# Pairing score units on TensorE in a fused cross-attention kernel, with a new order on every engine

## The reference

```python
q = _split_heads(hidden_states @ w_q, HEADS)
k = _split_heads(text @ w_k, HEADS)
v = _split_heads(text @ w_v, HEADS)
out_text = _merge_heads(_sdpa(q, k, v))
k_ip, v_ip = _split_heads(ip_h @ w_k_ip, HEADS), _split_heads(ip_h @ w_v_ip, HEADS)
out_ip = _merge_heads(_sdpa(q, k_ip, v_ip, mask=mask_ip))
out = (out_text + IP_SCALE * out_ip) @ w_out + b_out + residual
```

## Time and profile before

| | |
|---|---|
| median of 3 runs | 820.23 us (819.54 to 821.26) |
| the profiled execution | 820.14 us, its span 818.3 us |
| busy in the span | PE 795.8, DVE 676.2, POOL 627.7, ACT 541.3 us |
| stage 7 (its first pair to the next stage's) | 422.47 to 467.61 us |

### The profile page before, as it was taken

How to read it: one execution, slowest core, us unless ns; L and a number is a source line. 1 busy time by engine, 2 the same in 40 slices (tenths; PEclk the granted TensorE clock), 3 DMA queues, 4 the chain that set the end, 5 groups by cost and what they waited for, 6 DMA issues and landing times.

```text
span 818.3 us, 12921 instructions
## 1 busy us (share of the span) xinstructions
PE 795.8 (97%) x4381; PEld 648.8 (79%) x4381; DVE 676.2 (83%) x983; ACT 541.3 (66%) x928; POOL 627.7 (77%) x576
## 2 busy tenths in 40 slices
PE   9999889999999999999999999999999999999687
PEld 8889767888888878888787888878787887887466
DVE  6838767889878897889878888889888987888973
ACT  7766376677586667666785767676676757675632
POOL 0049648797987888797979888787979898788962
PEclk9999989999999999999999999999999999999999
DMA  9933587564767577764766487766766476465654
GB/s 314 391 125 113 175 271 235 179 230 141 240 213 220 189 231 219 231 213 140 265 182 212 160 255 220 223 201 183 253 192 243 130 240 211 155 194 180 194 185 162
DMA packets 104177, 169.99 MB, mean 208 GB/s; under 512 B 13104, under 2 KB 56112, under 8 KB 103984
## 3 DMA queue, kind: packets, MB, share of 16 engines
q1 hardware_dynamic: 103968, 167.86, 63.9%
q10 hardware_dynamic: 144, 1.31, 0.4%
HBM read 103.26 MB, written 65.54 MB: 206 GB/s over the span
## 4 chain that ended last, share of the span: by engine, by line
PE 88%; POOL 3%; DVE 3%; ACT 2%; SPq 1%; DMA 1%; issue 1%; DVEq 0%; ACTq 0%
PE bank L101 23%; PE bank L102 21%; PE bank L103 21%; PE bank L197 10%; PE bank L1176 4%; PE bank L1177 4%; PE bank L1061 1%; PE bank L1069 1%; PE bank L1073 1%; POOL prob L246 1%; POOL oT_lo L579 1%; DMA xin<-in_xT 1%; POOL pT_lo L583 1%; DVE wo_lo L846 1%; POOL prob L253 1%
## 5 line engine op out<-in xcount | busy, mean ns | idle before, releaser
L735 ACT ACTIVATE pv_part<-bank 64x512 f32<-64x512 f32 x160 | 94.7, 592 | 173.5 <-PE bank L1177 171.1
L246 POOL TENSOR_TENSOR prob<-prob,top 128x896 f32<-128x896 f32 (+1 forms) x160 | 184.0, 1170 | 14.8 <-DVE top L217 14.7
L253 POOL TENSOR_TENSOR prob<-prob,inv 128x896 f32<-128x896 f32 (+1 forms) x160 | 170.3, 1086 | 11.6 <-DVE inv L225 10.4
L101 PE MATMUL bank<-oT_hi,wo_hi 128*128 128x512 f32 x400 | 165.9, 415 | 3.6 <-POOL oT_lo L579 3.6
L966 DVE TENSOR_TENSOR o_raw<-bank,pv_part 64x512 f32<-64x512 f32 x160 | 110.1, 688 | 63.0 <-ACT pv_part L735 59.7
L101 PE MATMUL bank<-xT_hi,wq_hi 128*128 128x512 f32 x400 | 156.6, 392 | 2.6 <-DVE v_ip L938 2.6
L102 PE MATMUL bank<-oT_lo,wo_hi 128*128 128x512 f32 x400 | 157.7, 394 | 0.0
L103 PE MATMUL bank<-oT_hi,wo_lo 128*128 128x512 f32 x400 | 157.6, 394 | 0.0
L102 PE MATMUL bank<-xT_lo,wq_hi 128*128 128x512 f32 x400 | 156.1, 390 | 0.0
L103 PE MATMUL bank<-xT_hi,wq_lo 128*128 128x512 f32 x400 | 156.1, 390 | 0.0
L579 POOL TENSOR_TENSOR oT_lo<-o_raw,oT_hi 128x512 fp32r<-128x512 f32 x80 | 110.5, 1381 | 54.2 <-ACT oT_hi L739 52.5
(11 more groups left out here) (103 smaller groups left out, 1229.5 us busy)
## 6 DMA issues: line engine op xcount, KB each, us to landing
p_scratch<-stage SPq DMA_DIRECT2D x80, 512.0 KB, 3.0
prob<-p_scratch SPq DMA_DIRECT2D x320, 128.0 KB, 3.1
res<-in_xT SPq DMA_DIRECT2D x80, 256.0 KB, 4.7
outT<-res SPq DMA_DIRECT2D x80, 256.0 KB, 3.9
xin<-in_xT SPq DMA_DIRECT2D x75, 256.0 KB, 4.8
w_raw<-in_L_xattn_w_k SPq DMA_DIRECT2D x8, 320.0 KB, 5.6
w_raw<-in_L_xattn_w_k_ip SPq DMA_DIRECT2D x8, 320.0 KB, 6.2
w_raw<-in_L_xattn_w_v_ip SPq DMA_DIRECT2D x8, 320.0 KB, 4.3
```

Of the source, the lines that this page charges most:

```text
L101: nc.tensor.matmul(dst, a_hi, b_hi, start=first, stop=False)
L246: ins = nc.gpsimd.tensor_tensor(s, s, top[:, m, n, :].unsqueeze(2).broadcast_to([P, ROWS, k1 - k0]), ALU.subtract)
L253: ins = nc.gpsimd.tensor_tensor(s, s, inv[:, m, n, :].unsqueeze(2).broadcast_to([P, ROWS, k1 - k0]), ALU.mult)
```

## The change

Score units 1 and 2, and 3 and 4, stand directly behind each other on PE, between the third and fourth step (of five) of the query chunk of the same s, or where there are no queries, behind the outputs. Units 1 and 3 are written into the values banks, units 2 and 4 into `l_bank` as before; so unit 1 waits until DVE has added pairs 2 and 3, and pair 4 until unit 1 is copied. The copies of chunks 2 and 4 now wait until the group before has been read out of that chunk. Every engine has another order: the exponential, sums and maximum subtraction of chunk 4 move into the stage of its scores, the normalisation and transpose of chunk 3 to the start of the next. SP hands over chunks 0, 1 and 2 one by one, and 3 and 4 together ahead of the stores. No instruction that computes is added or taken away.

```diff
--- before.py
+++ after.py
         def s_bank(g, n):
-            return bank[n % 6] if g == 0 else l_bank[n % 2]
+            if g == 0:
+                return bank[n % 6]
+            return (v_bank if n // 2 in (1, 3) else l_bank)[n % 2]
...
         def copy_scores(act, g, m):
+            if g > 0 and m in (2, 4):
+                act.wait_ge(pT_lo_dve, KD * (g - 1) + m + 1)
+                act.wait_ge(pT_lo_pool, KD * (g - 1) + m + 1)
...
@@ sync, the loop over g
+                    hand_over(g, (3, 4) if g > 0 else (4,))
                     if g > 0:
                         for m in OUT_ORDER:
                             store(g - 1, m)
-                    hand_over(g, (4,))
...
                     if g + 1 < NG:
-                        hand_over(g + 1, (0, 1))
-                        hand_over(g + 1, (2, 3))
+                        for m in range(3):
+                            hand_over(g + 1, (m,))
...
@@ vector, the loop over g (its first part)
                         x_lo_part(dve, x, 2)
                     if g > 0:
+                        turn(dve, g, 3)
                         output(g - 1, 3)
                     if more_x:
                         x_lo_part(dve, x, 3)
+                    if more:
+                        maxima(dve, n, 0)
+                    turn(dve, g, 4)
+                    if more_x:
+                        x_lo_part(dve, x, 4)
                     if g > 0:
-                        sums(dve, g, 4)
                         output(g - 1, 4)
+                    pT_part(g, 4)
+                    if g > 0:
                         output(g - 1, 0)
-                    if more:
-                        maxima(dve, n, 0)
-                    if g > 0:
                         output(g - 1, 1)
                         output(g - 1, 2)
-                    if more_x:
-                        x_lo_part(dve, x, 4)
...
@@ tensor
                     wait(pe, pv_added, n - 1)
+                    if p // 2 in (2, 4) and g + 1 < NG:
+                        pe.wait_ge(score_copied, UNITS * (g + 1) + p - 1)
...
@@ next_scores(g, m)
+                    elif m in (1, 3):
+                        pe.wait_ge(pv_added, PAIRS * (g - 1) + 2 * m + 2)
                     else:
-                        if m == 1 and g > 1:
+                        if m == 2 and g > 1:
                             pe.wait_ge(out_done, outs_before(g - 2, 4) + 1)
-                        pe.wait_ge(score_copied, UNITS * g + 2 * m)
+                        pe.wait_ge(score_copied, UNITS * g + 2 * m - 2)
...
@@ the loop over g
                     for s in range(1, KD):
                         pv_pair(g, 2 * s)
                         pv_pair(g, 2 * s + 1)
-                        if g + 1 < NG:
-                            next_scores(g + 1, s)
                         wide_outs(g, s - 1)
-                        if g + 2 < NG:
+                        more_x, half = g + 2 < NG, 3 if s % 2 else KD
+                        if more_x:
                             if s == 1:
                                 wait(pe, out_done, outs_before(g - 1, 3) + 1)
                             pe.wait_ge(q_moved, KD * (g + 1) + KD - 1 if s == 1 else KD * (g + 2) + s - 1)
-                            q_steps(pe, g + 2, s - 1)
+                            q_steps(pe, g + 2, s - 1, 0, half)
+                        if s % 2 and g + 1 < NG:
+                            next_scores(g + 1, s)
+                            next_scores(g + 1, s + 1)
+                            if more_x:
+                                q_steps(pe, g + 2, s - 1, half, KD)
```

88 lines of the change are left out of this document (42 added, 46 removed).

## The result

The changed kernel takes **900.56 us** (median of 4 runs, 899.27 to 902.63); the kernel before, on the same chip, 819.88 (817.85 to 821.26). The ratio is 1.0987, with a 95% interval of 1.0966 to 1.1008. It is slower, as forecast, but by 80 us and not by 18, and 48 us beyond the end of the range. The profiled execution took 902.63 us, 82.5 more than the 820.14 of before.

What follows compares the result with a forecast made beforehand. PE, busy 97%, was taken as the bound in stages with query steps. 820.1 - 9.2 + 18.2 + 10.5 + 1.2 - 3 = 837.8, so 838 us; range 829 to 847 from its terms, 822 to 853 with most rivals.

Steps and rivals of the forecast that it cites:

- merged units: Two score units standing together on PE save 0.33 us a merge, 0.66 a stage, 9.2 in all.
- early wait: PE's first output step, behind pairs 2 and 3, waits for DVE's output 0: 1.4 us a stage (0.9 to 2.4), 18.2 in all.
- late wait: PE's unit 0 waits for ACT's last move of q: 1.5 us per even stage, 0.2 per odd; 10.5 and 1.2 in all.
- last two stages: Stages 14 and 15, where PE waits for others: the new order gives 3 us back, between 0 and 7.
- the x part at 435.62: Earlier-trace DVE step that met POOL's subtraction and took 1.08, not 0.65 us; model for x part 4's meeting.
- What costs nothing: Waits of units 1 and 3, pair 4, chunk copies, hand-overs, stores and loads are covered; chunk 1's hand-over just hidden: 0 us.
- The rule beside it: Skill's rule: issue order decides whether DVE or POOL blocks; taken strictly, early wait 2.4 us, some 852 in all.
- the row at 437.22: Earlier-trace DVE low part that took 0.67 us while POOL's pT_lo, issued 0.29 earlier, was stretched from 1.29 to 2.13.
- A: Rival: DVE loses both meetings with POOL in the early stretch, 1.0 us more a stage: 853; chance 0.16.
- B: Rival: the waits don't arise, 810, faster; needs both waits together under 0.66 us a stage; chance 0.12.
- C: Rival: only one of the early and late waits arises: 826, or 820 without the early one; chance 0.12.
- D: Rival: the merged units don't get cheaper on PE: 847; chance 0.03.

Runs made afterwards that it cites:

- kernel 6: Kernel 5, but SyncE hands over chunk 3 and then chunk 4, each with its own write and reads; 820.9 us.
- 7: Kernel 6, but three query matmuls stand between the two score units of each pair, so each unit is alone again; 828.8 us.
- Kernel 2: The changed kernel, but on DVE the maxima of chunk 0 stand ahead of the low part of x chunk 3; 874.6 us.
- kernel 3: The changed kernel, but ACT does build_k behind the high parts of pairs 0 and 1, not ahead of them; 901.8 us.
- 1: The changed kernel, but on DVE the low part of pair 4 stands behind outputs 0 to 2; 863.6 us.
- 4: Kernel 2, but on DVE outputs 4, 0, 1, 2 also stand ahead of chunk 4's transpose and the low parts of x 4 and pair 4; 882.6 us.
- 5: The edits of kernels 4 and 3 together on the changed kernel; 863.7 us.
- kernel 9: Kernel 6, but on ACT the move of q 3 and the exponential of chunk 4 stand ahead of the high part of pair 2; 833.1 us.
- kernel 11: Kernel 6, but SP issues the next batch's k and v loads behind chunk 0's hand-over, not ahead of all hand-overs; 829.9 us.

## Why the prediction was wrong

By its own parts, in us; what was measured is from the rows of windows and the waits above:

| term | forecast | measured |
|---|---|---|
| merged units | -9.2 | -9.6 |
| early wait | +18.2 | +43.4 |
| late wait | +11.7 | +12.8 |
| half clock | no term | +31.3 |
| head and stage 0 | 0 | +1.0 |
| last two stages | -3 | +3.6 |
| sum | +17.7 | +82.5 |

The two columns don't cover quite the same stages: the forecast's first and third terms have a part in stage 0, which is measured in the row of the head. With the wait of 1.79 there, the late waits come to 14.5, and stage 0's other steps to -0.8. The forecast's own range, 829 to 847, is also narrower than the bounds of its terms, which add up to 826 and, with the early wait of 2.4, to some 856; the measured time lies far outside either.

**What bounds the kernel** was read rightly, and so was the warning that a wait put on PE is paid in full; it is paid more than in full.

**Standing together**: right, 0.37 to 0.39 a merge for 0.33 (kernels 6, 7).

**The early stretch** is one of the two steps that failed, by its size. The place, the releaser and DVE's order were right. The step "the x part at 435.62 took 1.08 and not 0.65" took one meeting with POOL and let two others pass at their shortest; the upper bound of 2.4 took two. All three subtractions met POOL, and one of them took 2.20, twice the meeting in the earlier trace rows; from start to start the three took 4.67 us where 2.3 was counted. Kernel 2 shows that this is the meeting and not the operation. The forecast's own schedule held the longest meeting: it has x part 3 on DVE from 6.88 to 7.48 and POOL's normalisation of chunk 4 from 5.74 + 1.25 = 6.99 on, and it priced no meeting there. In the trace POOL was ahead by 0.06 us (466.85 against 466.91), so the subtraction was held for nearly all of POOL's first instruction. It was not bad luck: the normalisation of chunk 4, the maximum subtraction of chunk 0 and the `pT_lo` follow one another closely on POOL in this stretch, and eleven of the thirteen stages have the wait of 3.56 to 3.61. In the other two (1.98 and 2.01), half clock on PE had held up DVE's output 3 by 0.9, the subtraction came 0.94 or 0.95 us into POOL's operation, and it took 1.28 and 1.30.

**The late stretch**: right. 1.79 where 1.5 was counted, 0.17 to 0.54 where 0.2; kernel 3 shows that `build_k` is its cause. POOL's subtraction took 2.50 instead of 2.05 in it.

**The clock** is the other step that failed: the sum had no term for it. For waits of 1.4 and 1.5 us the trace of before gave none: its waits of 1.00 and 1.96 us in stage 14 were followed by the full clock. For longer ones it held a hint. Behind the idle of 3.95 in the earlier trace rows its view by windows has the clock at 0.56:

```profile
780.70:784.50 3.80, 3.80 (x11) 2.92 (x11) 3.12 (x4) 2.23 (x4) 3.75 (x4) 0.56 0.36 126
```

So the missing term hangs in good part on the wait that was too small: a wait of 3.6 in every stage should have been priced with it, and it came to 31.3 / 13 = 2.4 us a stage more. That the clock follows the waits is shown by kernels 1 to 6: no matmul differs between them, and busy time above 577 falls from 31 to 15 (kernels 2, 4), 10 (1, 5) and 0 (6) as the waits go; in kernel 3, where the long waits stay, it is 38.

**What costs nothing**: for the stores, loads and units of the changed kernel, as said. But two covers on SP's side were thinner than counted. "Chunk 1's hand-over ... just hidden" fails in four stages of kernel 6, where ACT waits 1.0 to 2.2 us for it and PE 1.3 to 2.05. And the joint hand-over had slack only because DVE's transpose of chunk 4 stood early; it tied chunk 3 to it. As long as PE waited 3.6 at the output step neither could be seen on PE.

**The last two stages**: wrong. From unit 0 of stage 14 on, before and after:

```profile
739.40:818.30 78.90, 62.64 (x306) 48.36 (x305) 57.43 (x79) 37.18 (x62) 53.17 (x48) 0.96 0.56 184
```

```profile
818.27:900.80 82.53, 66.42 (x305) 50.48 (x305) 54.75 (x78) 37.21 (x61) 51.66 (x48) 0.89 0.55 175
```

The idle time is 16.3 and 16.1, so nothing of the 3 us was saved; the 3.6 lost are clock again, 0.89 for 0.96.

**The rule beside it.** POOL was issued first in all three meetings (466.85, 470.37 and 472.84 against 466.91, 471.37 and 473.20) and DVE was held off in all three, which is what the Trainium skill, "SBUF — State Buffer", section "Who interferes with whom", says of two SBUF inputs. By this trace the rule was the better guide than the row at 437.22, which stays unexplained. For this case it gives no length for the block, and the 2.4 worked out from it was still 1.2 short.

**Rivals.** A was the nearest in kind, with two meetings in place of three and no clock. B came near only in kernel 6, where the waits fell to 10.3 / 13 = 0.79 a stage, just over the 0.66 (measured 0.74) from which it decides, and there it is a draw. C and D fell.

**What stays open**: what makes chunk 1 late in four stages (the loads ahead of it in the queue are ruled out; kernel 9 took its effect away without testing its cause, and each kernel has one trace); behind which waits the longer runs of kernel 11 lose their clock; and why the half clock follows some waits of about 2 us and not others of the same length.

## What to carry to other kernels

When an edit packs one engine's work more tightly, write the new order of all engines on one time line, and wherever a DVE subtraction of two SBUF tiles starts inside a POOL operation, let it end behind POOL's, by 0.55 us for the 128x512 tiles of this kernel; moving one of them past a reduction can be worth more than the edit itself (26 us against 9.6 here). On a kernel whose PE is fed without a gap, a forecast wait wants a second price for the clock behind it, read from the longest idle time in the trace that had none. And a wait that is removed uncovers the next one: joint hand-overs in a DMA queue tie the earlier chunk to the later one and cost nothing only until then.
